# Attention node stage: VectorE takes z first and the ending chain last in each step, ScalarE and GpSimd ordered to match

## What is computed

```python
h = jnp.maximum(_layernorm(x), 0.0)                     # h, of the node's x
z = layer_norm(h, ln1_g, ln1_b)                         # z
skip = z @ Wskip.T + bskip
out = segment_sum(a[:, :, None] * v_j, dst)             # agg, from the edge stage
beta = sigmoid(concatenate([out, skip, out - skip]) @ Wbeta.T)
y = h + beta * skip + (1.0 - beta) * out                # x_l
z2 = layer_norm(y, ln2_g, ln2_b)
y = y + relu(z2 @ W1.T + b1) @ W2.T + b2                # two-layer MLP, 128 -> 512 -> 128
x1 = x + y                                              # written to x1_table
h2 = jnp.maximum(_layernorm(x1), 0.0)                   # times 1/sqrt(degree), written to h2_table
```

## Time and profile before

| | before |
|---|---|
| median of 3 runs | 3553.65 us (3546.07 to 3562.57) |
| the profiled execution | 3554.38 us |
| its span, first to last instruction | 3552.5 us |
| mean granted TensorE clock over the span | 0.842 |
| busy: TensorE matmul, weight load | 2248.5, 1803.6 us |
| busy: VectorE, ScalarE, GpSimd | 2280.3, 1722.7, 2301.1 us |

### The profile page before, as it was taken

The page is one execution under the profiler, slowest core; times in us unless marked ns, Lnnn a source line. Parts: engine busy times, 40 slices in busy tenths (PEclk is TensorE's granted clock), DMA queues, the critical chain, the costliest instruction groups (busy, mean ns, idle before and its releaser), DMA issues. The chain is left out here.

```text
span 3552.5 us, 56630 instructions
## 1 busy us (share of the span) xinstructions
PE 2248.5 (63%) x13730; PEld 1803.6 (51%) x13730; DVE 2280.3 (64%) x9173; ACT 1722.7 (48%) x4075; POOL 2301.1 (65%) x2429
## 2 busy tenths in 40 slices
PE   0002777777777773799999999997443442455554
PEld 0002667766667762566666666665333332444444
DVE  8886666666666664677877787775111111678778
ACT  8994333333333331678887888886111111344343
POOL 5554777777777771555555555551777775777776
PEclk9998999999999995899999999999555555555555
DMA  6553233333333332233333333341566664456676
GB/s 204 177 176 94 82 101 92 91 101 91 91 101 91 91 101 62 65 105 107 107 100 102 108 104 102 101 109 67 124 129 130 132 131 113 118 149 152 144 147 133
DMA packets 253888, 401.93 MB, mean 113 GB/s; under 512 B 56515, under 2 KB 165456, under 8 KB 253728
## 3 DMA queue, kind: packets, MB, share of 16 engines
q1 hardware_dynamic: 183670, 265.77, 25.2%
q0 software_dynamic: 63424, 133.57, 18.6%
q10 hardware_dynamic: 6682, 1.46, 0.2%
HBM read 241.74 MB, written 160.29 MB: 113 GB/s over the span
## 5 line engine op out<-in xcount | busy, mean ns | idle before, releaser
L1159 POOL DMA_INDIRECT agg<-rows,at_n x392 | 388.8, 992 | 144.4 <-issue 111.1
L1651 POOL DMA_INDIRECT aggc<-rows,at_nc x392 | 398.8, 1017 | 113.2 <-issue 104.8
L628 POOL DMA_INDIRECT zs<-z_table,at_s x392 | 381.0, 972 | 112.9 <-issue 104.7
L628 POOL DMA_INDIRECT zd<-z_table,at_d x392 | 375.0, 957 | 119.4 <-issue 105.7
L1476 POOL DMA_INDIRECT h2s<-h_table,at_s x392 | 372.8, 951 | 113.2 <-issue 90.9
L1224 PE MATMUL p_f<-z_t,w_t 128*128 128x512 f32 x784 | 377.4, 612 | 64.1 <-ACT act L1294 64.0
L1529 PE MATMUL p_sum<-h2s,same 128*128 128x129 f32 x784 | 208.1, 438 | 307.8 <-DMA h2s<-h_table,at_s 244.4
L1235 PE MATMUL p_f<-w_t,act 128*128 128x128 f32 x3136 | 383.8, 278 | 0.0
L1235 PEld LDWEIGHTS p_f<-w_t,act 128*128 128x128 f32 x3136 | 361.2, 192 | 22.2 <-issue 22.2
L1529 PEld LDWEIGHTS p_sum<-h2s,same 128*128 128x128 f32 x784 | 173.3, 318 | 342.5 <-issue 264.8
L1516 DVE TENSOR_SCALAR same<-dst_sb,dst_g 128x128 f32<-128x128 uint16 x392 | 84.0, 303 | 400.8 <-DMA dst_sb<-dst 392.5
(11 more groups left out here) (317 smaller groups left out, 6471.9 us busy)
## 6 DMA issues: line engine op xcount, KB each, us to landing
rows<-rows_sb SPq DMA_DIRECT2D x49, 576.0 KB
h_table<-h2b SPq DMA_DIRECT2D x49, 516.0 KB, 2.9
rows<-rows_sb SPq DMA_DIRECT2D x49, 516.0 KB
xa<-in_x_dram SPq DMA_DIRECT2D x49, 512.0 KB, 3.8
z_table<-za SPq DMA_DIRECT2D x49, 512.0 KB, 2.9
dst_sb<-dst SPq DMA_DIRECT2D x98, 256.0 KB
xb<-in_x_dram SPq DMA_DIRECT2D x49, 512.0 KB, 4.0
x_table<-x1b SPq DMA_DIRECT2D x49, 512.0 KB, 4.7
```

What stands on the lines that cost most here:

```text
L628: pool.indirect_dma_start(out=to[:, slot, k], out_offset=None, in_=z_table, in_offset=bass.IndirectOffsetOnAxis(ap=at[:, slot, k:k + 1], a ...
L1159: pool.indirect_dma_start(out=agg[:, ring, k], out_offset=None, in_=rows0, in_offset=bass.IndirectOffsetOnAxis(ap=at_n[:, ring, k:k + 1], ...
L1651: pool.indirect_dma_start(out=agg[:, slot, k], out_offset=None, in_=rows1, in_offset=bass.IndirectOffsetOnAxis(ap=at_n[:, slot, k:k + 1], ...
```

## The change

Three engines' `half` of the attention node stage get another order. No instruction is added or taken away, and no instruction's shape changes.

- **VectorE** (L1348 on). Before: table copy, evacuate(1), the whole ending chain up to `var3`, logits, denominators, gate chain to `var2`, z, offset of norm2, norm3, evacuate(0). After: table copy, evacuate(1), **z**, logits, denominators, gate chain to `var2`, then **the x1 add and the statistics of x1**, the offset of norm2, the aggregation and `var3`, evacuate(0), norm3.
- **ScalarE**: the exponential moves from ahead of the relus to behind the second relu. The end of its step becomes h tiles 0 to 3, `copy_z(0)`, h tiles 4 to 7, `copy_z(1)`, z2 half 0, z2 half 1.
- **GpSimd**: all eight gathers first, then the power of `var2`, then that of `var3`.

```diff
@@ -1168,19 +1168,17 @@
...
-                            gather(ring, range(0, 3))
+                            gather(ring, range(G))
+                        if gating:
+                            g, slot, use, *_ = gating
+                            pool.wait_ge(S["var2"], g + 1)
+                            at_least(pool, S["z2_ready"], 2 * (g - 1))
+                            nc.gpsimd.tensor_tensor(norm2[:, slot, 0], var2[:], half_neg[:, 0:G], ALU.pow).then_inc(S["rstd2"], 1)
                         if ending:
                             g, slot, use, *_ = ending
                             pool.wait_ge(S["var3"], g + 1)
                             at_least(pool, S["h2_ready"], g - 1)
                             nc.gpsimd.tensor_tensor(norm3[:, slot, 0], var3[:], half_neg[:, 0:G], ALU.pow).then_inc(S["rstd3"], 1)
-                        if load:
-                            gather(load[3], range(3, G))
-                        if gating:
-                            g, slot, use, *_ = gating
...
                     flow(pool, half)
...
-                    def h_of(g, slot, use, ring, lap):
...
+                    def h_of(g, slot, use, ring, lap, tiles):
+                        if 0 in tiles:
+                            act.wait_ge(x_in[ring], 16 * (lap + 1))
+                            act.wait_ge(S["tab_ready"], g + 1)
+                            at_least(act, S["base_ready"], g - WAYS + 1)
+                            at_least(act, S["z_ready"], 2 * (g - WAYS + 1))
+                        for k in tiles:
                             last = a.activation(h_sb[:, ring, k], x_sb[:, ring, k], ACT.Relu, bias=norm[:, ring, 1, k:k + 1], scale=norm[:, ring, 0, k:k + 1])
-                        last.then_inc(S["h_ready"], 1)
+                        if G - 1 in tiles:
+                            last.then_inc(S["h_ready"], 1)
...
@@ -1309,27 +1309,28 @@
                             h2_of(last[0], last[1], last[2], range(4))
                         if mlp:
                             copy_z2(mlp[0], 1)
-                        if gating:
-                            act.wait_ge(S["logit_ready"], 3 * gating[0] + 3)
-                            a.activation(gate_e[:], logit[:], ACT.Exp, scale=-1.0).then_inc(S["gate_exp"], 1)
                         for q in range(2):
                             if mlp:
                                 at_least(act, S["f2_done"], 2 * (mlp[0] - 1) + q + 1)
                             for c in range(4):
                                 if mlp:
                                     relu(mlp[0], q, c)
+                                if gating and q == 0 and c == 1:
+                                    act.wait_ge(S["logit_ready"], 3 * gating[0] + 3)
+                                    a.activation(gate_e[:], logit[:], ACT.Exp, scale=-1.0).then_inc(S["gate_exp"], 1)
                                 if last and c % 2 == 1:
                                     h2_of(last[0], last[1], last[2], (4 + 2 * q + c // 2,))
                         if load:
-                            h_of(*load)
+                            h_of(*load, range(4))
+                        if prep:
+                            copy_z(prep[0], 0)
+                        if load:
+                            h_of(*load, range(4, G))
+                        if prep:
+                            copy_z(prep[0], 1)
                         if gating:
                             z2_of(gating[0], gating[1], gating[3], 0)
-                        if prep:
-                            copy_z(prep[0], 0)
-                        if gating:
                             z2_of(gating[0], gating[1], gating[3], 1)
-                        if prep:
-                            copy_z(prep[0], 1)
                     flow(act, half)
...
@@ -1353,20 +1354,15 @@
                         if ending:
                             g, slot, use, ring, lap = ending
                             evacuate(g, slot, use, ring, 1)
-                            dve.wait_ge(S["y_ready"], 2 * g + 2)
-                            v.tensor_tensor(x1_sb[:, slot], x1_sb[:, slot], x_sb[:, ring], ALU.add).then_inc(S["x1_ready"], 1)
...
-                            v.tensor_scalar(var3[:], mv3[:, :, 1], EPS, None, ALU.add).then_inc(S["var3"], 1)
+                        if prep:
+                            g, slot, use, ring, lap = prep
+                            dve.wait_ge(S["tab_ready"], g + 1)
+                            dve.wait_ge(S["h_ready"], g + 1)
+                            for q in range(2):
+                                at_least(dve, S["zt_turned"], 2 * (g - 1) + q + 1)
+                                for k in range(4 * q, 4 * q + 4):
+                                    last_ = v.tensor_scalar(z_sb[:, k], h_sb[:, ring, k], norm[:, ring, 2, k:k + 1], norm[:, ring, 3, k:k + 1], ALU.mult, ALU.add)
+                                last_.then_inc(S["z_ready"], 1)
                         if gating:
                             g, slot, use, ring, lap = gating
                             dve.wait_ge(S["wa_ready"], 2 * g + 2)
@@ -1419,20 +1415,32 @@
                             dve.wait_ge(S["bn2"], 2 * g + 2)
                             at_least(dve, S["rstd2"], g)
                             v.tensor_scalar(var2[:], mv2[:, :, 1], EPS, None, ALU.add).then_inc(S["var2"], 1)
-                        if prep:
...
-                                last_.then_inc(S["z_ready"], 1)
+                        if ending:
+                            g, slot, use, ring, lap = ending
+                            dve.wait_ge(S["y_ready"], 2 * g + 2)
+                            v.tensor_tensor(x1_sb[:, slot], x1_sb[:, slot], x_sb[:, ring], ALU.add).then_inc(S["x1_ready"], 1)
...
+                            last_.then_inc(S["bn3"], 1)
                         if gating:
                             g, slot, use, *_ = gating
                             dve.wait_ge(S["rstd2"], g + 1)
                             v.scalar_tensor_tensor(norm2[:, slot, 1], mv2[:, :, 0], -1.0, norm2[:, slot, 0], ALU.mult, ALU.mult).then_inc(S["norm2_ready"], 1)
                         if ending:
+                            g, slot, use, ring, lap = ending
...
+                            v.tensor_scalar(var3[:], mv3[:, :, 1], EPS, None, ALU.add).then_inc(S["var3"], 1)
+                        if mlp:
+                            g, slot, use, ring, lap = mlp
+                            evacuate(g, slot, use, ring, 0)
+                        if ending:
...
-                        if mlp:
-                            g, slot, use, ring, lap = mlp
-                            evacuate(g, slot, use, ring, 0)
                     flow(dve, half)
```

More of the change, by code:

```diff
@@ L1176, in half @@
                             nc.gpsimd.tensor_tensor(norm3[:, slot, 0], var3[:], half_neg[:, 0:G], ALU.pow).then_inc(S["rstd3"], 1)
-                        if load:
-                            gather(load[3], range(3, G))
-                        if gating:
-                            g, slot, use, *_ = gating
-                            pool.wait_ge(S["var2"], g + 1)
-                            at_least(pool, S["z2_ready"], 2 * (g - 1))
-                            nc.gpsimd.tensor_tensor(norm2[:, slot, 0], var2[:], half_neg[:, 0:G], ALU.pow).then_inc(S["rstd2"], 1)
                     flow(pool, half)
@@ L1421, in half @@
                             v.tensor_scalar(var2[:], mv2[:, :, 1], EPS, None, ALU.add).then_inc(S["var2"], 1)
-                        if prep:
[L1423 to L1429, removed]
-                                last_.then_inc(S["z_ready"], 1)
+                        if ending:
+                            g, slot, use, ring, lap = ending
+                            dve.wait_ge(S["y_ready"], 2 * g + 2)
+                            v.tensor_tensor(x1_sb[:, slot], x1_sb[:, slot], x_sb[:, ring], ALU.add).then_inc(S["x1_ready"], 1)
+                            dve.wait_ge(S["x1_ready"], g + 1)
+                            for k in range(G):
+                                last_ = v.bn_stats(six3[:, k], x1_sb[:, slot, k])
+                            last_.then_inc(S["bn3"], 1)
                         if gating:
@@ L1434, in half @@
                             v.scalar_tensor_tensor(norm2[:, slot, 1], mv2[:, :, 0], -1.0, norm2[:, slot, 0], ALU.mult, ALU.mult).then_inc(S["norm2_ready"], 1)
+                        if ending:
+                            g, slot, use, ring, lap = ending
+                            dve.wait_ge(S["bn3"], 2 * g + 1)
+                            hold(dve, held)
+                            for k in range(G):
+                                last_ = v.bn_aggr(mv3[:, k], six3[:, k])
+                            last_.then_inc(S["bn3"], 1)
+                            dve.wait_ge(S["bn3"], 2 * g + 2)
+                            at_least(dve, S["rstd3"], g)
```

(4 more changed lines are left out.)

## The result

| | before | after |
|---|---|---|
| median | 3555.08 us (3546.07 to 3562.57, 4 runs) | 3787.12 us (3779.81 to 3791.15, 4 runs) |
| profiled execution, span | 3552.5 us | 3785.9 us |
| granted TensorE clock, whole span | 0.842 | 0.817 |

The change makes the kernel slower: ratio 1.0648, 95% interval 1.0627 to 1.0669. The span is 233.4 us longer, and 226.6 of that lie in the attention node stage: the stage behind it starts its first load at 2710.98 us instead of 2484.40, and both kernels start this stage within 0.2 us of each other. The other 6.8 us lie behind this stage, in code that nobody touched; the executions of the kernel before alone differ by 16.5 us.

A forecast was written before the change was run, and what follows sets the result against it. It took the step as TensorE's work plus a 1.36 us hole, and after the change as a loop through the late x load: 3554.4 + 224 (loop) + 9 (clock) - 5 (ends) = 3782 us, range 3720 to 3880.

The forecast's parts named there:

- the loop: Attention node stage: x1 add releases x load, then h, z2, exponential; 25.9 us a step, 4.97 longer, 224 us in all.
- the table: Loop times after the exponential's start: x1 add ends 9.80, h starts 14.15, copy_z2(0) 21.29, next exponential 25.9 us.
- The clock, 9 us: TensorE's 4.3 us hole before its second transposition of z lowers its clock: 0.2 us a step, 45 steps.
- The ends of the stage, -5 us: Last five steps, without load, close the 1.36 us hole; first steps get z earlier: together -5 us.
- ScalarE's wait for x: At h (L1272), a wait for the x transfer of 4 to 5 us in each of 45 steps.
- What the change removes, 65 us: TensorE's 1.36 us wait for ScalarE's relus, late behind the exponential, closes in about 48 steps: 65 us.
- the first rival: Attention node stage: hole closes and load is not late; 19.4 us a step, 75 us less, 3480 us; 4%.

The follow-up runs named there:

- the early add: The changed kernel with the x1 add (and x1_ready) moved back directly behind evacuate(1), ahead of z: 3546.2 us, 0.9963 of the kernel before.
- the eight buffers: The changed kernel with eight buffers for x instead of four, the x1 add left late: 3555.7 us, 1.0014 of the kernel before.
- the extra add: The changed kernel with one more add of the same size on VectorE just ahead of the late x1 add: 3843.5 us, 1.0798.
- z2 ahead of h: The changed kernel with ScalarE taking both copies of z and both halves of z2 before h, x1 add still late: 3750.7 us, 1.0543.

## Why the prediction was right, and where it was not

The forecast was 3782 us, the time is 3787 us.

- **What bounds the changed kernel, and the loop.** Right. In the step shown the load's issue follows the add by 0.25 us, the load lands in 4.0 (the median), and h starts 14.17 us after the exponential (14.15 in the table). In the step before it, h starts at 2004.63, and from there to the next exponential it takes 2016.30 - 2004.63 = 11.67 us, for 11.75; in the step shown, with more time at 1.2 GHz, it takes 12.35. That the load is the cause is shown twice over, by the early add and by the eight buffers, and that VectorE's chain is on the loop by the extra add. z ends 2.7 us ahead of the next exponential and not 4, which still hides it.
- **The clock, 9 us.** Right in kind: the wait of 4.4 us is the one I had at 4.3, and the clock fell in each of 35 steps. Its price in the changed kernel stays between next to nothing (medians) and 0.30 us a step (profiled executions), for my 0.2, so that term is neither confirmed nor refuted. My reason for the low end was weak: I compared busy shares with the stage that keeps its clock, and yet the clock fell in every step. TensorE is busy 83%, not 75%, as the matmuls at 1.2 GHz take longer. The slack behind the hole probably kept the price low, though that wasn't tested by itself; with z2 ahead of h, where the turn and the skips lie on the loop, the unfilled steps lose 25.04 - 23.65 = 1.4 us to it on average. The Trainium skill (TensorE: Matmul & The Clock Gate, Part 1) describes a kernel whose TensorE falls back to the lower clock at each wait for a transfer. The changed kernel's 35 of 35 steps agree; with z2 ahead of h and a wait of 3.4 us it is 25 of 37.
- **The ends of the stage, -5 us.** The sum is near, the parts are not, and that is luck. The first x1 store comes at 1482.1 us for 1470.8, 11.3 us later, because that first add is late too; between the loads of steps 4 and 48 lie 44 steps x 5.1 = 224 us; in the last steps 8.6 us come back. Together 226.6 in the stage, for my 228. I had expected the first steps to gain. The sum's lower bound was miswritten as well: 3554.4 + 200 is 3754 and not 3745.
- **ScalarE's wait for x.** I wrote 4 to 5 us a step; it is 7.7. The relus and h2 end near 6.3 us after the exponential and h starts at 14.2, so my own table gave 7.9; I had subtracted wrongly. No term of the sum used it.
- **What the change removes, 65 us, and the first rival's 3480 us.** Wrong, in the step from "the hole of 1.36 us should close" to 65 us of gain. The hole closed, but the step that I had read as TensorE's work plus this hole was set by VectorE's chain to z too: the exponential alone gave 0.9994, as z took the hole's place. And with the load in time the changed kernel takes 3546 to 3556 us, since ScalarE's new tail delays z2. The rival asked only what the hole costs and not what is late next. It had 4%, so the forecast didn't suffer; had the load been in time, I would have promised 75 us and got at most 14 (3559.9 to 3546.2).

## What to carry to other kernels

When an instruction is moved within a hand-ordered step, list everything that its semaphore releases, on queues that the change doesn't touch too: here one add freed a buffer, and behind the buffer stood a transfer with 6.4 us of cover that went out 12.5 us later in the step (9.84 us behind the exponential, for 2.65 ahead of it). A hole in the busiest engine is worth only what the next constraint leaves: find the one that arrives just in time behind it, and test each half of an idea alone. If the load must stay late, more buffers bought back all of the loss here (eight for four), and work that doesn't need the load, placed ahead of the wait, a part.

## What the runs showed of the hardware

- In the changed kernel TensorE waits about 4.4 us once in each step of 26, and in each of 35 steps its clock falls to 1.2 GHz for 3.4 or 6.8 us, though the engine is busy 83% of the stage. With z2 ahead of h the wait is 3.4 us, and the clock falls in 25 of 37 steps. Filling the hole with 4.18 us of matmuls held the granted clock at 1.00 in both. What the fall costs differs with what follows the hole: 0.30 us a step in the changed kernel, by one execution of each version and not seen in the medians, and 1.4 where the turn and the skips behind it lie on the loop.
- GpSimd's power of eight columns (L1176) takes longer beside VectorE's add of two SBUF tiles than beside its statistics (or beside z, 1.70 us in the kernel before). The three groups are from the changed kernel, from the one with eight buffers for x (1500 to 2350 us) and from the one with the add early:

```profile
L1176 POOL TENSOR_TENSOR norm<-var,half_neg 128x8 f32<-128x8 f32 x27 | 67.6, 2505 | 262.8 <-DVE var L1417 262.8
```

```profile
L1184 POOL TENSOR_TENSOR norm<-var,half_neg 128x8 f32<-128x8 f32 x41 | 103.3, 2518 | 177.3 <-DVE var L1425 177.3
```

```profile
L1176 POOL TENSOR_TENSOR norm<-var,half_neg 128x8 f32<-128x8 f32 x34 | 57.0, 1675 | 141.5 <-DVE var L1419 141.5
```

  2505 and 2518 ns with the add right behind var2, 1675 without. The Trainium skill (GPSIMD Engine Reference, Specifications) says that the two engines share their SBUF interfaces and contend when VectorE reads two SBUF inputs; these rows agree, 0.83 us beside an add of 1.22. In the changed kernel ScalarE takes up z2 some 7 us after the offset that this power feeds is done, so it was off the path there.
